# Exponentials of one head for four tiles of a step, in place of two heads for two

## The reference

```
q, k, v = X@Wq+bq, X@Wk+bk, X@Wv+bv            # 16 heads of 16
attn = softmax(q k^T / 4) v ;  y = layernorm(X + attn@Wo + bo)
h = silu((y@w_gate)*s_gate) * ((y@w_up)*s_up)
out = layernorm(y + (h@w_down)*s_down)
```

## Time and profile before

| what | us |
|---|---|
| median of 3 runs | 612.54 (611.81 to 612.61) |
| the profiled execution | 611.91 |
| its span, first to last instruction | 610.1 |
| TensorE matmul busy | 596.8 (98%) |
| ScalarE busy | 510.8 (84%) |
| VectorE busy | 386.4 (63%) |
| GpSimd busy | 55.8 (9%) |
| granted TensorE clock, mean | 0.994 of full |

### The profile page before, as it was taken

The page is one execution under the profiler, slowest core; times in us unless marked ns, Lnnn a source line. Parts: engine busy times, 40 slices in busy tenths (PEclk is TensorE's granted clock), DMA queues, the critical chain, the costliest instruction groups (busy, mean ns, idle before and its releaser), DMA issues.

```text
span 610.1 us, 9962 instructions
## 1 busy us (share of the span) xinstructions
PE 596.8 (98%) x3952; PEld 252.3 (41%) x3952; DVE 386.4 (63%) x508; ACT 510.8 (84%) x586; POOL 55.8 (9%) x51
## 2 busy tenths in 40 slices
PE   8998999999999999999999999999999999999994
PEld 7892222222222323222223232222323226978874
DVE  6672000656666757786875658677757785777875
ACT  4538999999999999999999999999999996253351
POOL 6607000000000000000000000003000001102021
PEclk9998999999999999999999999999999999999998
DMA  9668882211102010101111111112010000101102
GB/s 218 115 102 104 123 113 34 34 26 18 28 11 65 8 31 8 31 7 33 48 28 21 20 22 17 27 12 64 9 32 8 5 5 9 39 0 37 35 0 70
DMA packets 36180, 24.67 MB, mean 40 GB/s; under 512 B 24930, under 2 KB 30946, under 8 KB 35538
## 3 DMA queue, kind: packets, MB, share of 16 engines
q1 hardware_dynamic: 34932, 23.42, 22.5%
q10 hardware_dynamic: 1200, 0.59, 0.4%
HBM read 6.56 MB, written 4.33 MB: 18 GB/s over the span
## 4 chain that ended last, share of the span: by engine, by line
PE 94%; DVE 2%; ACT 1%; DMA 1%; issue 1%; ACTq 0%; POOLq 0%; POOL 0%; DVEq 0%
PE ps L1195 41%; PE ps L1169 30%; PE ps L1300 10%; PE ps L1041 5%; PE ps L1277 4%; PE ps L1217 3%; ACT probs L624 1%; DMA x_tok<-in_L_attn_X 1%; DVE attn_q L779 1%; PE ps L1235 1%; PE ps L1027 1%; DVE stats L983 0%; DVE r_tmp L980 0%; DVE xt_lo L684 0%; DVE r_tmp L977 0%
## 5 line engine op out<-in xcount | busy, mean ns | idle before, releaser
L624 ACT ACTIVATE probs<-ps 128x1024 f32<-128x1024 f32 x484 | 448.3, 1117 | 21.5 <-PE ps L1169 21.5
L1195 PE MATMUL ps<-probs,v_all 128*17 128x512 f32 x1936 | 269.9, 600 | 1.3 <-ACT probs L624 0.3
L1169 PE MATMUL ps<-q_slot,k_stack 51*128 51x512 f32 x1024 | 206.1, 468 | 1.6 <-ACT probs L624 1.6
L1169 PEld LDWEIGHTS ps<-q_slot,k_stack 51*128 51x128 f32 x1024 | 87.7, 184 | 232.7 <-ACT probs L624 219.4
L858 DVE SCALAR_TENSOR_TENSOR poly<-poly,mant 128x1024 f32<-128x1024 f32 x84 | 102.9, 1225 | 2.9
L843 DVE TENSOR_SCALAR bits<-ps 128x1024 int32<-128x1024 f32 x28 | 34.3, 1224 | 72.6 <-PE ps L1169 72.6
L779 DVE COPY attn_q<-ps 128x512 f32<-128x512 f32 x16 | 11.1, 691 | 98.6 <-PE ps L1195 98.6
L643 ACT ACTIVATE sg<-ps,sgate_c 128x512 f32<-128x512 f32 x32 | 22.0, 689 | 49.5 <-PE ps L1300 49.5
L1195 PEld LDWEIGHTS ps<-probs,v_all 128*17 128x17 f32 x1936 | 33.6, 95 | 72.3 <-issue 55.0
L540 POOL TENSOR_TENSOR rstd<-var_eps,minus_half 128x4 f32<-128x4 f32 x4 | 4.1, 1022 | 378.7 <-DVE var_eps L811 378.7
L862 DVE SCALAR_TENSOR_TENSOR poly<-poly,bits 128x1024 f32<-128x1024 f32 x28 | 35.8, 1279 | 2.9
(11 more groups left out here) (95 smaller groups left out, 394.1 us busy)
## 6 DMA issues: line engine op xcount, KB each, us to landing
q_slot<-qy SPq DMA_DIRECT2D x64, 64.0 KB
k_stack<-k_part SPq DMA_DIRECT2D x12, 256.0 KB
at_dram<-attn_q SPq DMA_DIRECT2D x64, 34.0 KB
at<-at_dram SPq DMA_DIRECT2D x8, 272.0 KB, 2.9
q_slot<-qy SPq DMA_DIRECT2D x64, 32.0 KB
x_tok<-in_L_attn_X SPq DMA_DIRECT2D x14, 128.0 KB, 6.0
k_stack<-k_part SPq DMA_DIRECT2D x12, 128.0 KB
out<-out_tmp SPq DMA_DIRECT2D x12, 128.0 KB, 2.4
```

The lines of the kernel that those rows point to most:

```text
L624: nc.scalar.activation(probs[:, n % HALVES, :, :].rearrange("p a b -> p (a b)"), ps[:, 2 * ring:2 * ring + 2, :].rearrange("p a b -> p (a ...
L1169: last = nc.tensor.matmul(ps[:, 2 * ring + half, :], k_stack[s % QUADS][base:base + ROWS, p, kt * P:(kt + 1) * P], q_slot[slot][base:base ...
L1195: last = nc.tensor.matmul(ps[32 * hh:32 * hh + VW, ACC, :], v_all[:, tiles[hh // 2], NQ * (s % QUADS) + hh, :], prob, start=(kt == 0), sto ...
```

## The change

VectorE takes head 0 alone, for tiles 2, 6, 10 and 13 of every step from step 2 on, and for 10 and 13 in step 1. ScalarE takes head 1 of those pairs with half the width, and every pair has an instruction of it. Only head 0's value product has an order of its own. The polynomial is another form, with a square in it: r = (x+a)x; r = (r+b)r; line = (x+e)*scale; r = (r+c)*line; and the last product with the exponent. VectorE's results have six buffers, and the tiles `bits`, `mant` and `poly` are half as wide. A score pair waits for ScalarE and, where VectorE reads the one three before, for it too. VectorE's other work is spread over the gaps of four evaluations, and projections and transposes move by a unit or two.

```diff
-            return [] if s < 2 else [4, 11]
+            return [] if s == 0 else [10, 13] if s == 1 else [2, 6, 10, 13]
...
-            behind = {4: 9, 11: 15}
+            behind = {2: 5, 6: 9, 10: 13, 13: 15}
             late = {behind[kt]: kt for kt in poly_tiles(s)}
             others = [kt for kt in range(UPS) if kt not in poly_tiles(s)]
             return [late[i] if i in late else others.pop(0) for i in range(UPS)]
...
-            for n, g in enumerate(BY_ACT):
-                ring = g % 3
+            for g in range(2 * UPS * STEPS):
+                ring, first = g % 3, int(g in POLY_NO)
...
                 nc.scalar.activation(
-                    probs[:, n % HALVES, :, :].rearrange("p a b -> p (a b)"),
-                    ps[:, 2 * ring:2 * ring + 2, :].rearrange("p a b -> p (a b)"),
+                    probs[:, g % HALVES, first:2, :].rearrange("p a b -> p (a b)"),
+                    ps[:, 2 * ring + first:2 * ring + 2, :].rearrange("p a b -> p (a b)"),
                     ACT.Exp, bias=0.0, scale=SCALE).then_inc(exp_done, 1)
...
-                nc.vector.scalar_tensor_tensor(res[:], mant_f[:], QUARTER[4], mant_f[:], ALU.add, ALU.mult
-                                               ).then_inc(poly_step, 1)
-                for i in (3, 2, 1):
-                    dve.wait_ge(poly_step, 4 * n + 4 - i)
-                    nc.vector.scalar_tensor_tensor(res[:], res[:], QUARTER[i], mant_f[:], ALU.add, ALU.mult
-                                                   ).then_inc(poly_step, 1)
+                nc.vector.scalar_tensor_tensor(res, mant_f[:], POLY["a"], mant_f[:], ALU.add, ALU.mult
+                                               ).then_inc(poly_square, 1)
+                dve.wait_ge(poly_square, 2 * n + 1)
+                nc.vector.tensor_scalar(mant_f[:], mant_f[:], POLY["e"], POLY["scale"], ALU.add, ALU.mult
+                                        ).then_inc(poly_line, 1)
+                nc.vector.scalar_tensor_tensor(res, res, POLY["b"], res, ALU.add, ALU.mult
+                                               ).then_inc(poly_square, 1)
+                dve.wait_ge(poly_square, 2 * n + 2)
+                dve.wait_ge(poly_line, n + 1)
+                nc.vector.scalar_tensor_tensor(res, res, POLY["c"], mant_f[:], ALU.add, ALU.mult
+                                               ).then_inc(poly_cube, 1)
                 dve.wait_ge(poly_exponent, n + 1)
-                dve.wait_ge(poly_step, 4 * n + 4)
-                nc.vector.scalar_tensor_tensor(res[:], res[:], QUARTER[0], bits_f[:], ALU.add, ALU.mult
+                dve.wait_ge(poly_cube, n + 1)
+                nc.vector.scalar_tensor_tensor(res, res, POLY["d"], bits_f[:], ALU.add, ALU.mult
                                                ).then_inc(poly_done, 1)
...
+                exponentials(tiles[0])
                 if c >= 0 and stage == 1:
                     scale_attn(c)
                 if c >= 0 and stage == 2:
                     ln1_add(c, 0)
                 if c >= 0 and stage == 3:
                     ln1_add(c, 1)
+                if c >= 1 and stage == 0:
+                    ln1_parts(c - 1, 0)
+                exponentials(tiles[1])
+                if c >= 0 and stage == 3:
                     ln1_stats(c)
                 if c >= 1 and stage == 0:
-                    ln1_parts(c - 1, 0)
-                if tiles:
-                    exponentials(tiles[0])
+                    ln1_parts(c - 1, 1)
+                exponentials(tiles[2])
+                if c >= 0 and stage == 3:
+                    ln1_variance(c)
+                exponentials(tiles[3])
                 if c >= 0 and stage == 3:
                     ln1_scale(c)
...
-                elif g - 3 in POLY_NO:
-
-                    pe.wait_ge(poly_read, POLY_NO[g - 3] + 1)
                 else:
 
-                    pe.wait_ge(exp_done, ACT_NO[g - 3] + 1)
+                    pe.wait_ge(exp_done, g - 2)
+                    if g - 3 in POLY_NO:
+                        pe.wait_ge(poly_read, POLY_NO[g - 3] + 1)
...
-                tiles = [ORDER[s][kt], kt]
-                pairs = [2 * (UPS * s + tiles[p]) + p for p in range(2)]
-                pe.wait_ge(exp_done, 1 + max(ACT_NO[g] for g in pairs if g in ACT_NO))
+                tiles = [ORDER[s][kt], kt, kt, kt]
+                pairs = [2 * (UPS * s + tiles[hh]) + hh // 2 for hh in range(NQ)]
+                pe.wait_ge(exp_done, 1 + max(pairs[i] for i in range(NQ) if i or pairs[0] not in POLY_NO))
...
-                if c >= 0 and stage in (1, 2) and kt in (7, 15):
+                if c >= 0 and stage in (1, 2) and kt in (8, 15):
...
-                if c >= 1 and stage == 0 and kt in (1, 7):
+                if c >= 1 and stage == 0 and kt in (3, 8):
```

More of the change, by code:

```diff
@@ L41, in layer_program @@
     HALVES = 6
+    RESULTS = 6
     SCALE = float(HD) ** -0.5
@@ L44, in layer_program @@
     EPS = 1e-5
-    POLY = [0.497856220586085034, 0.355317066452090582, 0.105596708582285969, 0.0402255823502833695,
-            -0.000948847364620385358]
-    QUARTER = [p * 2.0 ** (2 * j - 1) for j, p in enumerate(POLY)]
+    POLY = dict(a=-1.7910860616458801, b=29.463461117307876, c=366.63643517373805, e=3.375058155969141,
+                scale=0.0009381183410730146, d=-0.9116985966799364)
     TO_BITS = SCALE * math.log2(math.e) * 2 ** 23
     LOWEST = -126.0 * 2 ** 23
-    FRACTION, FOURTH, EXPONENT, BIAS = 0x007FFFFF, 0x3E800000, 0x7F800000, 0x40000000
+    FRACTION, ONE, EXPONENT, BIAS = 0x007FFFFF, 0x3F800000, 0x7F800000, 0x40000000
     with ExitStack() as ctx:
@@ L119, in layer_program @@
         out_tmp = place("out_tmp", [P, TPC, HID], f32, at_parts + 28 * KB)
-        bits = place("bits", [P, 2, CW], i32, at_parts + 16 * KB)
-        mant = place("mant", [P, 2, CW], i32, at_parts + 20 * KB)
-        poly = [place(f"poly{i}", [P, 2, CW], f32, at_parts + 24 * KB + 4 * KB * i) for i in range(2)]
+        bits = place("bits", [P, CW], i32, at_parts + 16 * KB)
+        mant = place("mant", [P, CW], i32, at_parts + 18 * KB)
+        poly = place("poly", [P, RESULTS, CW], f32, at_parts + 20 * KB)
         at = region(32 * KB)
@@ L209, in layer_program @@
         poly_exponent = sem("poly_exponent")
-        poly_step = sem("poly_step")
+        poly_square = sem("poly_square")
+        poly_line = sem("poly_line")
+        poly_cube = sem("poly_cube")
         poly_done = sem("poly_done")
@@ L221, in layer_program @@
         ln1_sum = sem("ln1_sum")
+        ln1_stat = sem("ln1_stat")
         ln1_var = sem("ln1_var")
@@ L314, in layer_program, with poly_products @@
         POLY_NO = {g: n for n, g in enumerate(BY_POLY)}
-        BY_ACT = [g for g in range(2 * UPS * STEPS) if g not in POLY_NO]
-        ACT_NO = {g: n for n, g in enumerate(BY_ACT)}
+        def poly_products(g):
+            s, kt = g // 2 // UPS, g // 2 % UPS
+            return UPS * s + ORDER[s].index(kt) + 1
         def products_of(g):
-            s, kt = g // 2 // UPS, g // 2 % UPS
-            return UPS * s + (kt if g % 2 else ORDER[s].index(kt)) + 1
+            return g // 2 + 1
         def part_of(c, k, part):
@@ L615, in _ @@
             waited = 0
-            for n, g in enumerate(BY_ACT):
-                ring = g % 3
+            for g in range(2 * UPS * STEPS):
+                ring, first = g % 3, int(g in POLY_NO)
                 act.wait_ge(scores_ready, g + 1)
-                if n >= HALVES and products_of(BY_ACT[n - HALVES]) > waited:
-                    waited = products_of(BY_ACT[n - HALVES])
+                if g >= HALVES and products_of(g - HALVES) > waited:
+                    waited = products_of(g - HALVES)
                     act.wait_ge(pv_done, waited)
                 nc.scalar.activation(
-                    probs[:, n % HALVES, :, :].rearrange("p a b -> p (a b)"),
-                    ps[:, 2 * ring:2 * ring + 2, :].rearrange("p a b -> p (a b)"),
+                    probs[:, g % HALVES, first:2, :].rearrange("p a b -> p (a b)"),
+                    ps[:, 2 * ring + first:2 * ring + 2, :].rearrange("p a b -> p (a b)"),
                     ACT.Exp, bias=0.0, scale=SCALE).then_inc(exp_done, 1)
@@ L803, in ln1_stats, with ln1_variance @@
                     last = nc.vector.bn_stats(stats[:, TPC * c + j, :], x_by[:, j, c, :])
-                then(last)
+                last.then_inc(ln1_stat, 1)
+            def ln1_variance(c):
+                dve.wait_ge(ln1_stat, c + 1)
                 for t in range(TPC * c, TPC * (c + 1)):
@@ L833, in exponentials @@
                 g = BY_POLY[n]
-                ring, res = g % 3, poly[n % 2]
+                ring, res = g % 3, poly[:, n % RESULTS, :]
                 mant_f, bits_f = mant.bitcast(f32), bits.bitcast(f32)
@@ L842, in exponentials @@
                 dve.wait_ge(scores_ready, g + 1)
-                nc.vector.tensor_scalar(bits[:], ps[:, 2 * ring:2 * ring + 2, :], TO_BITS, LOWEST, ALU.mult, ALU.max
```

(41 more changed lines are left out.)

## The result

The changed kernel takes 620.77 us (median of 4, 620.29 to 621.71), the kernel before beside it 612.56. The ratio is 1.0133, with a 95% interval of 1.0118 to 1.0148: 1.3% slower. The forecast was 621.2, with a range of 616.0 to 626.5. The profiled execution took 621.71 us with a span of 619.9.

What follows compares the result with a forecast made beforehand. ScalarE's exponentials were taken to set plain attention steps, TensorE those with projections; step changes summed to +8.75 us, so 611.91 + 8.75 = 620.7 profiled, median 0.6 above: 621.2 us, range 616.0 to 626.5.

Steps and rivals of the forecast that it cites:

- TensorE waits in front of the product for place 12: Head 0's value product twelfth in its order, counted from 0, needs tile 14, two ahead: stall of 1.23 us per step.
- Its two terms: Exponential of pair 28 starts at 143.23, after the pair's 142.47; the product follows 1.14 later, at 144.37 instead of 143.14.
- pair 28: Score pair issued just in front of the product at place 12, whose exponential that product must wait for.
- ScalarE's loss: After the stall, pair 30 is read at 145.90 though ScalarE would be free at 145.06: 0.84 us lost in such a step.
- Half-width exponentials take 0.49: ScalarE, each half-width exponential 0.49 us; 28 full at 0.917 and 4 half make 27.64 a step, against 27.51 before.
- The two breaks go: ScalarE's two breaks of some 0.28 us behind skipped exponentials vanish: 0.56 us less in a plain step.
- By step: Attention steps 1 to 15: plain +0.41 each, step 1 +0.1, projection steps +0.84 or +0.65, transpose steps +0.85; sum 8.75 us.
- TensorE's sum: TensorE's work in a 16-tile step: 16 units of 1.65 us, given as 26.35, plus 0.23 at the border, 26.58.
- VectorE doesn't bound: VectorE's evaluations take 4.85 us, at most 5.3, four a step 19.4, with tiles 6.6, 6.6 and 4.95 us apart.
- 0.6 of lateness: VectorE's variance, 0.7 us before a step's last evaluation, makes that evaluation 0.6 us late, within about 1 us of slack.
- The moved pieces cost nothing: VectorE's other work between evaluations is hidden, and moved transposes and projections keep their data in time; uncovered, up to 0.7.
- The rival on the other side: ScalarE has finished pair 28 when the product comes, so only gains stand, 6.1 us together: 606.4 us; chance 0.09.

Runs made afterwards that it cites:

- tile 10 at place 12: Changed kernel with head 0's value product of tile 10 taken at place 12 instead of 13, never more than one ahead: 606.82 us, again 606.96 us.
- it at place 14: Changed kernel with tile 10 of head 0 at place 14 instead of 13, so places 12 and 13 are both two ahead: 642.03 us.
- the kernel before by the order alone: Kernel before, two wide VectorE tiles, with tile 4 at place 11 instead of 9, so place 10 needs tile 12, two ahead: 623.55 us.

## Why the prediction was right

The forecast was +8.75 in the attention. From the end of step 0 to the first feed-forward product it is 79.79 to 506.13 before and 80.98 to 515.97 after: 426.34 and 434.99, +8.65.

- *TensorE waits in front of the product for place 12.* Shown: 15 waits in the changed kernel, none of them with tile 10 at place 12, two a step with it at place 14, and the same wait in the kernel before by the order alone. Predicted late by 1.23, measured 1.16. Its two terms were off against each other: the exponential of pair 28 starts 0.54 after the pair where the prediction had 0.76 (143.23 less 142.47), and from its start to the product it is 1.29 (159.66 to 160.95), not 1.14. ScalarE's loss 0.84, measured 0.66 + 0.10 = 0.76.
- *Half-width exponentials take 0.49.* Measured 0.47 to 0.49. Hence 27.64 a step, and 27.63 where nothing else is in the way. The price from the Trainium skill (ScalarE: Activation LUTs, What ACT_TABLE_LOAD costs), 0.52, is a little high here: with four of them a step would be an estimated 27.76.
- *The two breaks go.* Shown by the run of 32 exponentials in one piece.
- *By step.* Plain 28.48 predicted, 28.39 and 28.40 measured in steps 2 to 4. Steps 7, 11 and 15 took 28.30, 28.31 and 26.91; they were shorter before too (27.81, 27.79 and 26.45, where the prediction put 28.07), and grew by 0.46 to 0.52, so that the six gave 2.45 for the 2.5 of the sum. Step 1 29.33, measured 29.24; steps 6, 10, 14 29.85, measured 29.87 to 29.88; steps 5, 9, 13 29.9, measured 29.98 to 29.99; steps 8 and 12 28.96, measured 28.82 to 28.83. Against before, steps 5, 9 and 13 grew by 2.2 in all (1.95 predicted), steps 6, 10 and 14 by 2.7 (2.5), steps 8 and 12 by 1.35 (1.7), and step 1 by nothing (0.1): the small errors cancel. A slip of 0.05 stands in TensorE's sum: 16 x 1.65 is 26.40, not 26.35.
- *VectorE doesn't bound.* An evaluation took 4.78 (139.22 to 144.00), 4.85 predicted. Its read starts 0.61 to 0.65 after the first matmul of its scores, or 0.75 behind the save of a step and 0.70 behind the variance, where the prediction had 0.6 of lateness; no wait of TensorE in the changed kernel ends with one of these reads.
- *The moved pieces cost nothing.* True within some 0.4 us, with the projections and transposes at either place. What I had not seen is how near step 1's first evaluation lay to the key loads: the tile that the prediction had near 98 is read at 96.08, and in another execution at 94.74, released by the keys.
- *What was partly luck.* The profiled executions differ by 9.8, not 8.65: 1.2 more is in step 0, which the change doesn't touch (it ended at 80.98 instead of 79.79, with TensorE's clock low for about 6.8 us instead of 3.4). The medians differ by 8.2. That the small errors by step, and the two terms of the wait, cancel is luck too.

The rival on the other side, that the look-ahead is hidden, was priced at 606.4. It is what the kernel takes once the look-ahead is really gone, 606.8 to 607.0.

## What to carry to other kernels

When work is put off in an in-order queue and other items fill its place, write the whole order out, and count for each place how far ahead it reaches of what the ring (here the three pairs of banks used in turn) already guarantees; one ahead was free here, two ahead cost 0.7 to 1.1 us each time. Such a cost does not show as load of any engine (TensorE's busy time even fell, from 596.8 to 590.7 us): compare the length of a step with the busiest engine's sum in it, and look for the one hole. With the order right, the changed kernel's median is 6.7 and 5.5 us below the kernel before in the two groups. In the traces the attention behind step 0 is 4.9 shorter; 0.85 of this is step 1, where ScalarE's work did shrink, and 4.1 came in steps 2 to 15 from splitting the relief into smaller pieces, because a piece no longer outran the ring. ScalarE's busy time hardly changed over these steps: it is 509.7 against 510.8 in all, with 0.85 of that in step 1.

## What the runs showed of the hardware

TensorE's clock. At the start of the attention, where TensorE waits for ScalarE between the first scores, the granted clock is at the lower level for a time that differs from execution to execution. Before, and after, in the profiled ones:

```profile
53.00:56.00 3.00, 3.00 (x24) 0.58 (x20) 0.00 (x0) 2.86 (x3) 3.00 (x4) 0.88 0.90 98
```

```profile
53.00:56.00 3.00, 3.00 (x14) 0.65 (x12) 0.00 (x0) 1.94 (x2) 3.00 (x3) 0.50 0.87 93
```

Over all traces the lower level lasts there 0, about 3.4 or about 6.8 us, and from the first exponential to its save step 0 takes 32.0, 32.7 to 32.8 or 34.0 us. So this is worth up to 2 us. It goes with the larger part of the spread of tile 10 at place 12 (606.27 to 608.61 over both groups): the two executions above 608 have a mean granted clock of 0.991, the nine others, 606.27 to 607.40, one of 0.993 to 0.997. The attention itself also starts at different times, 46.82 to 48.51. What decides either is open; it wasn't tried. One wait of 0.9 to 1.1 us per step never lowered the clock later on; two within 3 us did in 3 of 15 steps, and so did the wait of 6.4 us for the keys.

Two engines at once. The four 128x256 scalings of the layer norm take 1.38 us on VectorE when GpSimd is idle. In the last step of the changed kernel and its variants they run beside GpSimd's conversion of the down weights, and take twice as long: the second of the four takes 1.98 instead of 0.41, and ends 0.15 after the conversion (timeline of the kernel with tile 10 at place 12, GpSimd's row and VectorE's):

```profile
499.07 2.00 POOL L558 CAST wd<-down 128x2048 fp32r<-128x2048 int8 x1 [3.67 <-DVE poly L876]
```

```profile
498.92 2.94 DVE L828 TENSOR_SCALAR x_tok<-x_tok,mean_var,rstd 128x256 f32<-128x256 f32 x4
```

The save behind them is late by it, but TensorE goes on to the feed-forward part at 500.85 without it.
